# Packing the routing tasks of the last halves in a planned attention and expert kernel, and norming the last half's rows two tiles at a time

## The chip, the cores and the metric

The kernel runs on one core of a Trainium2 chip. The metric is the device time of one execution in microseconds. All engines of the core run their own instruction queues and meet by semaphores: TensorE (PE), VectorE (DVE), ScalarE (ACT), GpSimd (POOL) and SyncE (SP), which only issues transfers.

## The reference

Four sequences of 1,024 rows of 256 numbers (4,096 tokens) go through cross attention with a context, then through a mixture of experts. Cut to what matters:

```python
x = x + xattn(ctx, layernorm(x), mask, ...)     # q from x; keys and values from the context (77) and from x (1024)
h = layernorm(x)                                # "hn": the rows that are routed
scores = sigmoid(h @ gate_w.T)                  # 64 experts in 8 groups of 8
sfc = scores + gate_bias
# the 4 best groups by the sum of their two best, then the 8 best experts in them
topk_w = 2.5 * scores[topk] / (scores[topk].sum() + 1e-20)
pos = running count of an expert's tokens, in token order      # valid while pos < 256
buf[e, pos] = h[token]
y = (silu(buf @ w_gate) * (buf @ w_up)) @ w_down
out = x + sum over the valid choices of y[e, pos] * topk_w
```

Everything is in float32. An expert takes its first 256 tokens only, so the count runs through the halves in order.

## The kernel before

A sequence b has two halves x of 512 query rows, so there are eight halves, named (b, x); the last is (3,1). A half has two pairs pr of heads, and (b, x, pr) is a block. A block has 9 steps, one for each tile of 128 keys: `scores` (four matrix passes on TensorE, then `exp` on ScalarE into `probs`) and `values` (four passes into `ps_o`). Behind a block ScalarE copies the sums and the denominators out (`o_copy`, lines 1364 and 1365) and VectorE divides (`scale`, lines 1490 and 1491, in two pieces of 256 columns). A block needs the row maxima of its scores first: `max` (TensorE line 1097, VectorE line 1474) and `max_ctx`, then `neg` on VectorE, then `qb`, a transposition on TensorE (line 1124) that ScalarE copies to `qbT` (line 1334). Only then do its `scores` start.

When both blocks of a half are divided, the half is routed. Its tasks, in the order in which `route_tasks` gives them, with q one of its 4 tiles of 128 rows:

- `proj` for each tile (TensorE line 1167; VectorE lines 1496 to 1500: add to `xres`, mean and variance), then `store` (SyncE line 883: the rows go to the output)
- `hn_scale` in four pieces (VectorE: 1 / sqrt by a shift and three Newton steps, in `rsqrt`, for all four tiles at once) and `hn` for each tile (ScalarE line 1375: the normed rows into `rows`)
- `hn_turn` (TensorE line 1174, ScalarE line 1381) and `logits` (TensorE line 1180, ScalarE line 1387) for each tile
- the choice, 14 tasks on VectorE from `gates` (line 1515) to `scale_weights` (line 1598). `chosen` marks the experts, `count` adds up, `pos` (TensorE lines 1191 and 1193) gives the place of each token in its expert, `slots` and `slot_ids` make the addresses, and the last two make the weights
- 32 scatters on GpSimd (`scat`, line 956), 8 for each tile: an indirect transfer of 128 rows to `slot_rows` in memory. The first scatter of a tile waits for its choice and its normed rows.

Seven halves make one choice for their four tiles together. The last half makes four choices, one for each tile, so that its scatters can start with the first tile.

Behind the last half comes the expert stage. SyncE waits for all 256 scatters and loads the rows expert by expert (line 901); TensorE turns them and multiplies; GpSimd adds the results to the output with indirect transfers (line 1023), which wait for one another by `added0` and `added1`. The experts' weights come in three early groups: 16 behind block (2,1,1), 6 behind block (3,0,1), and 17 (line 898) behind the last block. The 17 are issued by SyncE behind the `store` of the last half, since they follow `plan.order["sp"]` in its queue.

The order of the work is made by `Plan` when the kernel is built. It puts each task in a slot (one `scores` or `values` task is a slot), beside a load in microseconds that it adds up for each engine. `route` places the routing tasks: for the halves up to (2,0) as a chain, by their costs; for (2,1) and (3,0) simply two tasks to a slot. Half (3,1) stands behind all slots. The list of all tasks gives the priorities. Then `schedule` gives each engine its own order: it takes, among the tasks whose needs (in `needs`, with assumed times) are met within 0.3 us of the soonest, the one that stands first in the list. The engines work through these orders strictly. TensorE's tasks other than `scores` and `values` share three banks of `ps_u` in turn.

## Time and profile before

| what | us |
|---|---|
| median of 3 runs | 1167.11 (1161.54 to 1170.71) |
| the profiled execution | 1164.94 |
| its span | 1163.0 |
| busy in it: PE, DVE, POOL, ACT | 945.4, 616.8, 587.2, 461.3 |
| 256 scatters (line 956), busy | 251.7, 983 ns each |
| 128 result transfers (line 1023), busy | 198.3, 1550 ns each |

The span is the time between the first and the last instruction that the profiler saw; the execution takes 1.9 us more. A row of the timeline has the start in us, the busy time in us, the engine, the line, the operation, what is written and what is read with shapes, and a count if it holds several like instructions. In brackets stand the idle time of the engine ahead of it and what ended it. "issue" means that the profile shows nothing that the engine waited for. PE is the matrix pass, PEld the load of its weights.

### The profile page before, as it was taken

The page shows a single profiled execution, that of the slowest core. Times are in us where ns is not written, and L with a number is a line of the kernel's source. Part 1 is how long each engine was busy: PE and PEld are TensorE (multiplying, and loading weights), DVE is VectorE, ACT ScalarE, POOL GpSimd, SP SyncE. Part 2 cuts the span into 40 slices and gives each one's busy share as a digit, 9 for nine tenths or more (in the row PEclk, how much of TensorE's full clock was granted, in tenths as well). Part 3 has the DMA queues.
Part 4 walks back from the last instruction along what each step waited for, and adds up shares of the span by engine and source line. Part 5 has one row for each costly group of instructions (what it writes and reads, how often), then busy time and mean ns, then how long its engine had stood idle before and what let it go on. Part 6 is the DMA issues. An engine that isn't in the chain of part 4 may idle for free.

```text
span 1163.0 us, 12926 instructions
## 1 busy us (share of the span) xinstructions
PE 945.4 (81%) x3736; PEld 598.3 (51%) x3736; DVE 616.8 (53%) x1898; ACT 461.3 (40%) x930; POOL 587.2 (50%) x530
## 2 busy tenths in 40 slices
PE   3779999999999999999999999961079977878700
PEld 1445565645655554555555545531068866666500
DVE  4473536896568776467857666647124323332300
ACT  3633665733856444566453432530023322222100
POOL 3620042307616625722853737276736667777782
PEclk9878999999999998999999998985579988998955
DMA  8519301113202323300124403015069987877668
GB/s 304 213 41 386 138 1 39 37 44 144 70 1 78 124 68 100 108 1 7 68 73 165 165 19 116 20 48 222 8 193 295 258 185 135 145 140 136 82 68 153
DMA packets 79285, 133.66 MB, mean 115 GB/s; under 512 B 13419, under 2 KB 48027, under 8 KB 79217
## 3 DMA queue, kind: packets, MB, share of 16 engines
q1 hardware_dynamic: 47345, 91.04, 23.9%
q0 software_dynamic: 31872, 41.80, 18.4%
q8 instruction: 31, 0.51, 0.2%
q14 instruction: 37, 0.30, 0.1%
HBM read 60.76 MB, written 93.00 MB: 132 GB/s over the span
## 4 chain that ended last, share of the span: by engine, by line
PE 57%; POOL 11%; issue 10%; DMA 9%; DVE 7%; ACT 4%; POOLq 0%; DVEq 0%; ACTq 0%; SPq 0%
PE ps_o L1158 22%; PE ps_u L1074 7%; PE ps_s L1142 6%; PE ps_s L1144 5%; DMA out_rows<-again,row_ids 5%; PE ps_u L1097 4%; POOL out_rows L1023 4%; POOL odd_sum L1023 3%; DMA odd_sum<-again,row_ids 3%; POOL slot_rows L956 3%; PE ps_u L1167 2%; PE ps_u L1085 2%; PE ps_u L1113 2%; PE ps_u L1124 1%; ACT den L1365 1%
## 5 line engine op out<-in xcount | busy, mean ns | idle before, releaser
L956 POOL DMA_INDIRECT slot_rows<-rows,slot_idx x256 | 251.7, 983 | 212.2 <-issue 182.7
L1474 DVE TENSOR_REDUCE mp<-ps_u 128x1 f32<-128x512 f32 x256 | 164.7, 686 | 107.4 <-PE ps_u L1097 105.7
L1348 ACT ACTIVATE probs<-ps_s 128x512 f32<-128x512 f32 x256 | 139.5, 596 | 160.0 <-PE ps_s L1144 158.5
L1158 PE MATMUL ps_o<-probs,V 128*128 128x512 f32 (+1 forms) x288 | 141.1, 614 | 2.9 <-ACT den L1365 2.9
L1158 PE MATMUL ps_o<-probs,pool 128*128 128x512 f32 (+1 forms) x288 | 140.5, 611 | 3.2 <-ACT den L1365 3.2
L971 POOL TENSOR_TENSOR pool<-pool,rs_y 128x1024 f32<-128x1024 f32 (+1 forms) x20 | 32.9, 1647 | 198.9 <-DVEq L1469 198.7
L1219 PE MATMUL ps_u<-again 128*128 128x256 f32 x512 | 130.1, 400 | 0.0
L1617 DVE TENSOR_SCALAR again<-ps_o,again 128x256 f32<-128x256 f32 x128 | 56.1, 480 | 138.8 <-DMA out_rows<-again,row_ids 79.1
L1023 POOL DMA_INDIRECT out_rows<-again,row_ids x64 | 99.2, 1550 | 53.4 <-DVE row_ids L1618 20.8
L1023 POOL DMA_INDIRECT odd_sum<-again,row_ids x64 | 99.1, 1549 | 37.0 <-issue 17.7
L1144 PE MATMUL ps_s<-qbT,Kb 65*128 65x512 f32 (+1 forms) x288 | 117.2, 407 | 0.0
L1219 PEld LDWEIGHTS ps_u<-again 128*128 128x128 f32 x512 | 99.4, 205 | 12.7 <-issue 0.3
L1074 PE MATMUL ps_u<-wqkv_s,lnT 128*128 128x512 f32 (+1 forms) x256 | 99.9, 521 | 3.0 <-ACT lnT L1271 1.9
L1394 ACT ACTIVATE again<-ps_s 128x512 f32<-128x512 f32 x64 | 38.2, 597 | 161.4 <-PE ps_s L1203 161.4
L1228 PE MATMUL ps_o<-again 128*128 128x256 f32 x256 | 71.3, 403 | 36.5 <-DVE again L1608 36.4
L1158 PEld LDWEIGHTS ps_o<-probs,V 128*128 128x128 f32 (+1 forms) x288 | 52.5, 193 | 48.0 <-issue 29.4
L1142 PE MATMUL ps_s<-Q,K 128*128 128x512 f32 x144 | 73.0, 507 | 4.3 <-ACT qbT L1334 4.3
L1158 PEld LDWEIGHTS ps_o<-probs,pool 128*128 128x128 f32 (+1 forms) x288 | 52.1, 193 | 46.8 <-issue 32.2
L1228 PEld LDWEIGHTS ps_o<-again 128*128 128x128 f32 x256 | 47.5, 194 | 52.6 <-DVE again L1608 47.0
L1203 PE MATMUL ps_s<-ident,again 128*128 128x128 f32 x256 | 41.9, 291 | 36.1 <-DMA again<-slot_rows 36.1
L1074 PEld LDWEIGHTS ps_u<-wqkv_s,lnT 128*128 128x128 f32 x256 | 49.2, 201 | 36.8 <-issue 27.1
L1490 DVE RECIPROCAL den<-den 128x256 f32<-128x256 f32 x32 | 55.9, 1747 | 17.5 <-ACT den L1365 17.1
(181 smaller groups left out, 1443.7 us busy)
## 6 DMA issues: line engine op xcount, KB each, us to landing
again<-in_wexp SPq DMA_DIRECT2D x64, 384.0 KB, 6.5
slot_rows<-rows SPq DMA_DIRECT2D x2, 10272.0 KB, 33.1
again<-slot_rows SPq DMA_DIRECT2D x64, 321.0 KB, 4.2
Kb<-K SPq DMA_DIRECT2D x16, 275.5 KB, 3.9
odd_sum<-rows SPq DMA_DIRECT2D x1, 4352.0 KB, 22.4
pool<-in_x SPq DMA_DIRECT2D x4, 1024.0 KB, 5.6
xres<-in_x SPq DMA_DIRECT2D x8, 512.0 KB, 3.8
out_rows<-xres SPq DMA_DIRECT2D x8, 512.0 KB, 3.0
```

The lines of the kernel that those rows point to most:

```text
L956: pool.indirect_dma_start(out=slot_rows, out_offset=bass.IndirectOffsetOnAxis(ap=slot_idx[x][:, q, k:k + 1], axis=0), in_=rows[x][:, q, :] ...
L1023: pool.indirect_dma_start(out=(out, odd_sum)[e % 2], out_offset=bass.IndirectOffsetOnAxis(ap=row_ids[:, e % RING, t:t + 1], axis=0), in_=y ...
L1074: i = pe.matmul(dst, lnT[0:w, at % 2, c, 0:rj], rhs, start=(c == 0), stop=(c == 1))
L1142: pe.matmul(dst, K[b % 2][:, h, kt * P:kt * P + rk], queries(b, x)[0][:, h, :], start=True, stop=False)
L1144: pe.matmul(dst, Kb[:, h, kt * P:kt * P + rk], qbT[block_no[(b, x, pr)] % 2][:, hh, :], start=False, stop=True).then_inc(s["scores_full"], 1)
L1158: i = pe.matmul(ps_o[:, hh, :], V[b % 2][0:rk, pr, kt, DH * hh:DH * hh + P], probs[0:rk, n % NPR, hh, :], start=(kt == 0), stop=(kt == NKT ...
L1219: i = pe.matmul(ps_g[:, e % 2, which, :], w_at[e % W_BUFS][:, o:o + I], xT[e % 2][:, k, :], start=(k == 0), stop=(k == 1))
L1228: i = pe.matmul(ps_y[:, e % 2, t, :], hid[e % 2][:, t * P:(t + 1) * P], w_at[e % W_BUFS][:, 4 * I:4 * I + D], start=True, stop=True)
L1348: act.activation(probs[:, n % NPR, hh, :], ps_s[:, u % NSC, :], ACT.Exp).then_inc(s["probs_made"], 1)
L1474: v.tensor_reduce(mp[:, i, tile, half:half + 1], bank((*t, i))[:, :], AX.X, ALU.max).then_inc(s["emptied_vec"], 1)
L1490: link(v.reciprocal(den[:, mine], den[:, mine]))
L1617: v.tensor_scalar(y_out[r][:, t, :], ps_y[:, e % 2, t, :], xr[r][:, t, D + 1 + e:D + 2 + e], None, ALU.mult)
```

## The change

It has four parts.

1. `route` puts four tasks of halves (2,1) and (3,0) to a slot instead of two.
2. The tasks of a half's rows are in a function of their own, `row_tasks`, for tiles q0 to q1, and `hn_scale` works on these tiles only. `NORMED` says that half (3,1) does it in two parts: tiles 0 and 1, then tiles 2 and 3.
3. The last half's list reads: first piece of the last block's `scale`, the rows of tiles 0 and 1, second piece of `scale`, the choice of tile 0 with its scatters, the rows of tiles 2 and 3, `store`, and the choices of tiles 1, 2 and 3 with theirs. Before it was: both pieces, the rows of all four tiles, the four choices.
4. In all other halves `store` stands behind `hn` in the list, not ahead of `hn_scale`.

The rest adapts `needs` and the waits: ScalarE waits for `hn_scaled` at the first tile of a part, and for `sel_made` by a part's number. `CHOSEN` is empty, so halves other than the last keep one choice.

```diff
+NORMED = {(B - 1, 1): ((0, 2), (2, 4))}
+CHOSEN = {}
...
-        for q in range(2):
-            self.add("scale", *order[-1], q)
...
-        for t in self.route_tasks(B - 1, 1, parts=[(q, q + 1) for q in range(QT)]):
+
+        rows_made = [self.row_tasks(B - 1, 1, *tiles) for tiles in NORMED[(B - 1, 1)]]
+        chosen = [[(kind, B - 1, 1, q, q + 1) for kind in CHOICE] + [("scat", B - 1, 1, q, k) for k in range(TOPK)]
+                  for q in range(QT)]
+        for t in ([("scale", *order[-1], 0)] + rows_made[0] + [("scale", *order[-1], 1)] + chosen[0] + rows_made[1]
+                  + [("store", B - 1, 1)] + chosen[1] + chosen[2] + chosen[3]):
             self.add(*t)
...
-                self.slots.setdefault(first + n // 2, []).append(t)
-            first += len(tasks) // 2
+                self.slots.setdefault(first + n // 4, []).append(t)
+            first += len(tasks) // 4
...
+    def row_tasks(self, b, x, q0, q1):
+
+        out = [("proj", b, x, t) for t in range(q0, q1)]
+        out += [("hn_scale", b, x, n, q0, q1) for n in range(4)]
+        out += [("hn", b, x, t) for t in range(q0, q1)]
+        for t in range(q0, q1):
             out.append(("hn_turn", b, x, t))
-            if t:
+            if t > q0:
                 out.append(("logits", b, x, t - 1))
...
+        return out + [("logits", b, x, q1 - 1)]
+
+    def route_tasks(self, b, x):
+        out = [t for tiles in NORMED.get((b, x), ((0, QT),)) for t in self.row_tasks(b, x, *tiles)]
+        last = out.index(("hn", b, x, QT - 1))
+        out[last + 1:last + 1] = [("store", b, x), ("residual", b, 1) if x == 0 else ("residual", b + 1, 0)]
+        for part in CHOSEN.get((b, x), ((0, QT),)):
             out += [(kind, b, x, *part) for kind in CHOICE]
         return out
...
-                    b, x, piece = t[1:]
+                    b, x, piece, q0, q1 = t[1:]
+                    mine = slice(q0, q1)
                     if piece == 0:
-                        if 2 * b + x:
+                        if 2 * b + x and q0 == 0:
                             v.wait_ge(s["hn_made"], QT * (2 * b + x))
-                        link(v.tensor_scalar(c_v[:], mvC[:, :, 1], LN_EPS, None, ALU.add))
-                    rsqrt(v, link, c_v[:], c_i[:], c_y[:], c_t[:], (piece,))
+                        link(v.tensor_scalar(c_v[:, mine], mvC[:, mine, 1], LN_EPS, None, ALU.add))
+                    rsqrt(v, link, c_v[:, mine], c_i[:, mine], c_y[:, mine], c_t[:, mine], (piece,))
```

What the plan makes of it is seen best in three places. Line numbers of the new kernel are higher, by 11 to 15.

ScalarE at the start of block (3,0,0), before: the copy of block (2,1,1) (`oT`, `den`) stands ahead of `qbT` of block (3,0,0).

```order
L1351 ACTIVATE probs<-ps_s,mask_bias 77x512 x2
L1364 ACTIVATE oT<-ps_o 64x512
L1365 ACTIVATE den<-ps_o 64x512
L1364 ACTIVATE oT<-ps_o 64x512
L1365 ACTIVATE den<-ps_o 64x512
L1334 ACTIVATE qbT<-ps_u 65x512 x2
L1348 ACTIVATE probs<-ps_s 128x512 x16
```

And in the changed kernel:

```order
L1363 ACTIVATE probs<-ps_s,mask_bias 77x512 x2
L1346 ACTIVATE qbT<-ps_u 65x512 x2
L1376 ACTIVATE oT<-ps_o 64x512
L1377 ACTIVATE den<-ps_o 64x512
L1376 ACTIVATE oT<-ps_o 64x512
L1377 ACTIVATE den<-ps_o 64x512
L1360 ACTIVATE probs<-ps_s 128x512 x12
```

`qbT` has moved ahead of the copy. On TensorE `qb` has moved ahead of the last `values` of block (2,1,1) in the same way. The same swap is at the start of block (2,0,0), and not at (3,1,0), where one pair of maxima has moved ahead of the last `values`.

VectorE in the middle of the choice of half (3,0), before: `selb` is written by `chosen`, `carry` by `count`, `wsel<-ps_u` is the first instruction that reads the positions, and `den` and `oT` are `scale` of block (3,1,0).

```order
L1556 MATCH_REPLACE rep<-v,sfc 128x64 x4
L1559 TENSOR_TENSOR selb<-rep,sfc 128x256
L1490 RECIPROCAL den<-den 128x256
L1491 TENSOR_TENSOR oT<-oT,den 128x256
L1562 TENSOR_TENSOR carry<-carry,selb 128x64 x4
L1490 RECIPROCAL den<-den 128x256
L1491 TENSOR_TENSOR oT<-oT,den 128x256
L1570 TENSOR_TENSOR wsel<-ps_u,slot_base 128x256
L1571 SCALAR_TENSOR_TENSOR rep<-ps_u,selb 128x256
```

And in the changed kernel:

```order
L1571 MATCH_REPLACE rep<-v,sfc 128x64 x4
L1574 TENSOR_TENSOR selb<-rep,sfc 128x256
L1577 TENSOR_TENSOR carry<-carry,selb 128x64 x4
L1585 TENSOR_TENSOR wsel<-ps_u,slot_base 128x256
L1586 SCALAR_TENSOR_TENSOR rep<-ps_u,selb 128x256
L1592 COPY carry<-carry 128x64
```

Both pieces of `scale` stand behind `scale_weights` now. On TensorE, all logits of the half stand ahead of `qb` of block (3,1,1) and of the `values` of step 6 of block (3,1,0); before, the last of them stood behind the `values` of step 7. Its `pos` stands ahead of the first `values` of block (3,1,1) instead of the fourth.

VectorE in the last half, before: `xres` is written by `proj`, with `bnC` and `mvC` behind it, and `c_v`, `c_i`, `c_y`, `c_t` and `c_nb` are `hn_scale`. These rows are the fourth `proj`, and what follows.

```order
L1496 TENSOR_TENSOR xres<-xres,ps_u 128x256
L1499 BN_STATS bnC<-xres 128x6
L1500 BN_AGGR mvC<-bnC 128x2
L1506 TENSOR_SCALAR c_v<-mvC 128x4
L580 TENSOR_SCALAR c_i<-c_v 128x4
L581 TENSOR_SCALAR c_y<-c_i 128x4
```

In the changed kernel, from the end of the first two tiles' `hn_scale` to the first choice (`sc` is `gates`):

```order
L1524 SCALAR_TENSOR_TENSOR c_nb<-mvC,c_y 128x2
L1510 TENSOR_TENSOR xres<-xres,ps_u 128x256
L1513 BN_STATS bnC<-xres 128x6
L1514 BN_AGGR mvC<-bnC 128x2
L1510 TENSOR_TENSOR xres<-xres,ps_u 128x256
L1513 BN_STATS bnC<-xres 128x6
L1514 BN_AGGR mvC<-bnC 128x2
L1521 TENSOR_SCALAR c_v<-mvC 128x2
L591 TENSOR_SCALAR c_i<-c_v 128x2
L592 TENSOR_SCALAR c_y<-c_i 128x2
L1530 TENSOR_SCALAR sc<-th 128x64
```

The third and fourth `proj` stand behind `hn_scale` of the first two tiles. The second piece of `hn_scale` of tiles 2 and 3 stands between `count` and `pos` of the first choice, and the last two pieces stand behind that choice. In this part of the program the orders of GpSimd and SyncE are the same in both kernels.

## Rows read from the trace of the kernel before

**Rows 1.** The page, its first line.

```profile
span 1163.0 us, 12926 instructions
```

**Rows 2.** The timeline of GpSimd and of SyncE's queue, from the scatters of (3,0) on.

```profile
758.54 0.99 POOL L956 DMA_INDIRECT slot_rows<-rows,slot_idx  x1 [18.46 <-issue]
...
799.33 0.98 POOL L956 DMA_INDIRECT slot_rows<-rows,slot_idx  x1 [5.02 <-issue]
...
842.08 0.98 POOL L956 DMA_INDIRECT slot_rows<-rows,slot_idx  x1 [1.96 <-issue]
...
845.93 0.98 POOL L956 DMA_INDIRECT slot_rows<-rows,slot_idx  x1 [0.30 <-issue]
848.09 3.90 SPq L901 DMA_DIRECT2D again<-slot_rows  x8
```

**Rows 3.** The timeline of GpSimd in the scatters of half (2,1).

```profile
727.79 0.98 POOL L956 DMA_INDIRECT slot_rows<-rows,slot_idx  x1 [3.16 <-issue]
```

**Rows 4.** DMA queues in 780 to 786, 786 to 794, and the loads' queue in 799.3 to 803.

```profile
q0 software_dynamic: 90, 0.13, 9.7%
...
q0 software_dynamic: 308, 0.04, 3.4%
...
q1 hardware_dynamic: 281, 0.74, 52.2%
```

**Rows 5.** The timeline of VectorE and TensorE, choice of half (3,0).

```profile
740.73 0.29 DVE L1515 TENSOR_SCALAR sc<-th 128x256 f32<-128x256 f32 x1 [8.11 <-ACT th L1387]
...
747.92 1.75 DVE L1490 RECIPROCAL den<-den 128x256 f32<-128x256 f32 x1
...
748.38 1.88 PE L1158 MATMUL ps_o<-probs,V 128*128 128x512 f32 x4
...
751.04 1.88 PE L1158 MATMUL ps_o<-probs,V 128*128 128x512 f32 x4
...
753.19 0.42 DVE L1570 TENSOR_TENSOR wsel<-ps_u,slot_base 128x256 f32<-128x256 f32 x1 [0.16 <-PE ps_u L1193]
```

**Rows 6.** The timeline of the last half: VectorE, and the weight loads.

```profile
770.71 1.75 DVE L1490 RECIPROCAL den<-den 128x256 f32<-128x256 f32 x1 [13.00 <-ACT den L1365]
...
778.05 0.42 DVE L1496 TENSOR_TENSOR xres<-xres,ps_u 128x256 f32<-128x256 f32 x1
...
780.06 10.30 SPq L898 DMA_DIRECT2D again<-in_wexp  x17
...
780.31 0.17 DVE L1506 TENSOR_SCALAR c_v<-mvC 128x4 f32<-128x4 f32 x1
...
782.71 0.16 DVE L1509 SCALAR_TENSOR_TENSOR c_nb<-mvC,c_y 128x4 f32<-128x4 f32 x1
...
786.77 0.20 DVE L1515 TENSOR_SCALAR sc<-th 128x64 f32<-128x64 f32 x1 [3.90 <-ACT th L1387]
...
794.30 0.15 DVE L1598 COPY rows<-token_id 128x1 f32<-128x1 f32 x1
```

**Rows 7.** The timeline at the starts of blocks (2,0,0), (3,0,0) and (3,1,0).

```profile
445.32 0.50 PE L1142 MATMUL ps_s<-Q,K 128*128 128x512 f32 x1 [2.50 <-ACT qbT L1334]
...
624.26 1.04 PE L1124 MATMUL ps_u<-ident,QL 128*65 128x128 f32 x8
...
624.46 0.59 ACT L1364 ACTIVATE oT<-ps_o 64x512 f32<-64x512 f32 x1 [3.36 <-PE ps_o L1158]
...
626.89 1.07 ACT L1334 ACTIVATE qbT<-ps_u 65x512 fp32r<-65x512 f32 x2
...
628.02 0.50 PE L1142 MATMUL ps_s<-Q,K 128*128 128x512 f32 x1 [1.81 <-ACT qbT L1334]
...
696.15 2.48 DVE L1474 TENSOR_REDUCE mp<-ps_u 128x1 f32<-128x512 f32 x4 [1.06 <-PE ps_u L1097]
```

**Rows 8.** Windows: length, busy PE, PEld, DVE, ACT, POOL, PEclk, DMA share, GB/s.

```profile
446.00:453.00 7.00, 7.00 (x14) 3.50 (x13) 3.85 (x5) 2.88 (x5) 5.44 (x6) 0.51 0.37 131
...
698.00:709.00 11.00, 10.17 (x28) 6.82 (x27) 6.75 (x11) 3.70 (x7) 8.56 (x9) 0.53 0.61 213
```

More of the change, by code:

```diff
@@ L154, in __init__ @@
                     self.add(*t)
-        for t in self.route_tasks(B - 1, 1, parts=[(q, q + 1) for q in range(QT)]):
+        rows_made = [self.row_tasks(B - 1, 1, *tiles) for tiles in NORMED[(B - 1, 1)]]
[3 more added lines that the diff above has]
+                  + [("store", B - 1, 1)] + chosen[1] + chosen[2] + chosen[3]):
             self.add(*t)
-            if t[0] == "scale_weights":
-                for k in range(TOPK):
-                    self.add("scat", B - 1, 1, t[3], k)
         self.schedule()
@@ L270, in add, with normed_with @@
         self.tasks.append((kind, *args))
-    def route_tasks(self, b, x, parts=((0, QT),)):
-        out = [("proj", b, x, t) for t in range(QT)]
-        out += [("store", b, x)] + [("hn_scale", b, x, n) for n in range(4)]
-        out += [("hn", b, x, t) for t in range(QT)]
-        if (b, x) != (B - 1, 1):
-            out.append(("residual", b, 1) if x == 0 else ("residual", b + 1, 0))
-        for t in range(QT):
+    def row_tasks(self, b, x, q0, q1):
[3 more added lines that the diff above has]
+        for t in range(q0, q1):
             out.append(("hn_turn", b, x, t))
-            if t:
+            if t > q0:
                 out.append(("logits", b, x, t - 1))
-        out.append(("logits", b, x, QT - 1))
-        for part in parts:
+        return out + [("logits", b, x, q1 - 1)]
[4 more added lines that the diff above has]
+        for part in CHOSEN.get((b, x), ((0, QT),)):
             out += [(kind, b, x, *part) for kind in CHOICE]
         return out
+    def normed_with(self, b, x, q):
+        return next(k for k in NORMED.get((b, x), ((0, QT),)) if k[0] <= q < k[1])
     def needs(self, t):
@@ L395, in needs @@
             yield "dve", 1.15, [(*t, "pe"), ("residual", b, x, "pool")] + (
-                [("hn_scale", c, y, 3, "dve")] if b + x else [])
+                [("hn_scale", c, y, 3, *self.normed_with(c, y, QT - 1), "dve")] if b + x else [])
         elif kind == "store":
@@ L399, in needs @@
         elif kind == "hn_scale":
-            b, x, piece = t[1:]
+            b, x, piece, q0, q1 = t[1:]
             c, y = (b, 0) if x else (b - 1, 1)
-            yield "dve", 0.65, [("proj", b, x, q, "dve") for q in range(QT)] + (
-                [("hn_scale", b, x, piece - 1, "dve")] if piece else
+            yield "dve", 0.65, [("proj", b, x, q, "dve") for q in range(q0, q1)] + (
+                [("hn_scale", b, x, piece - 1, q0, q1, "dve")] if piece else
                 [("hn", c, y, q, "act") for q in range(QT)] if b + x else [])
@@ L406, in needs @@
             b, x, q = t[1:]
-            yield "act", 0.42, [("hn_scale", b, x, 3, "dve")] + (
+            yield "act", 0.42, [("hn_scale", b, x, 3, *self.normed_with(b, x, q), "dve")] + (
                 [("scat", b - 1, x, QT - 1, TOPK - 1, "pool", 3.5)] if b else [])
@@ L425, in needs @@
             elif n == 0 and b + x:
-                done.append((CHOICE[-1], c, y, 0, QT, "dve"))
+                done.append((CHOICE[-1], c, y, *self.part_of[(c, y, QT - 1)], "dve"))
             if kind == "pos":
@@ L749, in program @@
     pos_units = [u for u in units if u[0] == "pos"]
+    scaled_no = {(t[4], *t[1:3]): n for n, t in enumerate(t for t in plan.tasks if t[0] == "hn_scale" and t[3] == 3)}
     part_no = {(*u[1:3], q): n for n, u in enumerate(pos_units) for q in range(u[3], u[4])}
```

11 lines of the change are left out of this document (6 added, 5 removed).

## The prediction

> **What bounds the kernel now.** I read the page first, then the timeline of GpSimd around the end of attention, then the instructions that feed it, and last the stretches in which TensorE waits or runs slowly. The span is 1163.0 us [rows 1]. It has two stages. In attention (up to the last `values` task) TensorE is busy nearly all the time. In the expert stage TensorE starts only when every routed row stands in `slot_rows`: SyncE issues the first load of rows at 848.09, directly behind the last scatter of GpSimd, which starts at 845.93 and takes 0.98 [rows 2]. From there to the end are 314.9 us that the change does not touch. So the question is when the last scatter ends.
>
> GpSimd issues the scatters of half (3,0) and then those of (3,1), 64 in all, from 758.54 on. They stand 1.285 us apart. The run has two gaps that are larger: 5.02 us before 799.33 and 1.96 us before 842.08 [rows 2]. The first comes behind the 28th scatter of (3,0), the second 32 scatters later. The same gap stands behind 28 scatters of half (2,1), with 3.16 us [rows 3]. I read it as a ring of 32 scatters: at its end GpSimd waits until the scatters under way have landed. Quiet, that costs about 2 us; in the 5.02 us case the 17 weight loads issued from 780.06 were running. In their first 6 us the scatters' queue moved 90 packets, 15 per us; in the next 8 us it moved 308, 38 per us [rows 4], which is what scatters 1.285 us apart ask for (49 each). So loads starve the scatters at first, and the backlog is gone only slowly. GpSimd, from 758.54 on, is thus the path, and what starts it is the choice of half (3,0).
>
> **The choice of (3,0): 8.7 us earlier.** Before, `gates`, the first step of the choice, waits 8.11 us for the last logits and starts at 740.73 [rows 5]. In the new order `qb`, two `values` tasks and one `scores` task that stood ahead of these logits stand behind them. A `scores` with its `values` takes 2.66 us (748.38 to 751.04 [rows 5]), a second `values` 1.9 and `qb` 1.04 [rows 7]: 5.6 us together. The normed rows must be ready in time for that. `hn_scale` now runs in one piece, with fewer maxima between its steps, which brings them about as much forward. I take 5.2 us, since TensorE may then wait a little for the first of them. Next: before, two `scale` tasks (one reciprocal 1.75 us and one product each, from 747.92) stood inside the choice; it reads the positions at 753.19 [rows 5], and 5.35 us later GpSimd starts. Now the choice runs as one piece and the scales stand behind it; nobody waits for them until the copy of the last block, 20 us later. From 747.92 to the positions it was 5.3 us; the two reciprocals (3.5 us) and about 0.4 of the products go from it, 3.9 us, and the count and the positions' matmul remain. TensorE reaches that matmul only behind the first `scores` tasks of the next block, which gives 0.4 us back. So 5.2 + 3.9 - 0.4 = 8.7: GpSimd starts at 749.8.
>
> **The gap at the ring's end: 0.5 us given back.** 28 scatters at 1.285 bring the gap to 785.8 instead of 794.3. Where are the weights then? They are issued behind the store of the last half, which waits for the fourth `proj`. That `proj` now stands behind the first two tiles' `hn_scale`, which takes from 780.31 to 782.87 [rows 6], 2.6 us, so the loads start at 782.7. The gap would fall 3 us into them, into the worst part. The backlog is then 3 us of (38 - 15), some 70 packets, and the scatter just issued, 49: 45 of them leave in the slow 3 us that remain, the rest at 38 per us in 1.9 us, and landing takes 0.4: a gap of 5.3 us. GpSimd goes on at 791.1 instead of 799.33, 8.2 us earlier. Bounds: with a gap of 2 us, as the quiet one, it goes on at 787.8 (11.5 earlier); if it waits until all 17 loads are in (about 21 us from their start), at 804, 4.7 later than before. I stay near the 5.02 us row, the one taken under the same loads.
>
> The 36 scatters that remain take 47.6 us from 799.33 on, with one quiet gap [rows 2]; the gap's place behind the loads is kept, so they cost the same. They need the first choice of (3,1) when four of them are done, at 796.2. Before, it is ready at 794.45 [rows 6]. Now two `proj` rounds (778.05 to 780.31, 2.26 us [rows 6]) leave its path, and one `hn_scale` piece of 0.6 us enters between count and positions, where VectorE waits for the matmul anyway. That makes 792.3: no wait. The later choices cost 7.6 us each (786.77 to 794.45 [rows 6]) and the next one 1.4 us more, against 10.3 us for eight scatters: covered. Without the split the choice would stand at 794.5, still ahead of 796.2, so by itself the split buys nothing with my gap, and 1.6 us with a quiet one. Its 13 more small VectorE instructions lie beside GpSimd and cost nothing; what it does cost is that the loads start 2.6 us later, which is in the gap above.
>
> A page bears on this and speaks against it. The Trainium skill, "SBUF — State Buffer", section "SBUF: two separate sides", says that GpSimd cannot write descriptors while VectorE holds the port pair that they share, so that choices beside scatters would stretch them. The trace does not agree: the scatters stand 1.285 us apart with VectorE idle (758.54 to 770.71) and with its choices running (799.33 on) [rows 2, 6]. By that rule the sum would be smaller by an amount that no row gives; I use the row.
>
> **Attention: 6.5 us earlier.** The end of attention moves all of the above. The `values` and `scores` tasks are the same in number, so only waits of TensorE can go. There are three places, each at the start of a block. At 624.46 ScalarE copies the finished block out, and only then, at 626.89, the `qb` result; TensorE stands 1.81 us and starts at 628.02 [rows 7]. In the new order `qb` is ahead of the last `values` on TensorE and ahead of the copy on ScalarE. Then `scores` follow the last `values` without a wait and the next `values` wait only for the copy: 2.3 us less. The same swap stands at block (2,0,0), where TensorE stands 2.50 us [rows 7]: again 2.4. At (3,1,0) four reductions (2.48 us from 696.15 [rows 7]) are between the last `values` and `qb`; one pair of them (1.3 us) has moved ahead: 1.3. The denser rows (three `proj` in a row, four logits in a row) can make TensorE wait for banks: minus 1. Sum 5.0, bounds 0 and 6.
>
> At two of the three places the clock fell just after the wait: 0.51 in 446 to 453 and 0.53 in 698 to 709, the lower level of 1.2 GHz [rows 8]; at 628, after 1.81 us, it did not. Half clock over 7 and 10 us of dense work costs 3.4 and 5. With shorter waits one of these may go; another may come where order is new. I add 1.5 us, with bounds of -4 and +8. The Trainium skill ("TensorE: Matmul & The Clock Gate", "What's actually happening") says the same from the other side: idleness throttles the clock and activity releases it. By that rule, taken strictly, both dips go, which is the upper bound; the row at 628 shows that a wait alone does not settle it.
>
> **Sum.** 8.2 (GpSimd against the end of attention) + 5.0 + 1.5 = 14.7 us. 1163.0 - 14.7 = 1148.3 of span; the execution took 1164.94, 1.9 above its span, so 1150.2. From the median of the three runs, 1167.11, it is 1152.4. I forecast 1151.
>
> **Rivals.**
> 1. *The gap swallows the loads.* GpSimd cannot go on before the weights are in. For it: in the first 6 us the scatters' queue got two fifths of its rate. Against: before, it went on at 799.33 while 281 load packets were still to come [rows 4]. Price: -4.7 instead of +8.2; the total gain is 1.8 and the time 1164. Chance 0.12.
> 2. *Attention does not gain.* The waits move elsewhere, since VectorE is nearly full around the packed rows, and a dip stays at each place. 1163.0 - 8.2 + 1.9, or 1159 from the median: about 1158. Chance 0.18.
> 3. *Both gains in full.* Quiet gap and both dips gone: 11.5 + 6 + 8 = 25: 1141. Chance 0.13.
> 4. *The swap turns against the kernel.* `qb` now stands ahead of the last `values` in TensorE's order. If the maxima end late, because a choice holds VectorE (it holds it 7.2 us up to `chosen`, 740.73 to 747.92 [rows 5]), TensorE stands with that `values`, the copy and the next block behind it. From a delay of some 4 us at each of the two swaps it eats the gain; with 6 us each and two further dips (3.4 and 5) it is 20 us lost against 8.2 won: 1178. For it: VectorE has to be through with the maxima one `values` earlier than before. Against: the positions of the choice (0.9 us), which stood ahead of the last maximum, stand behind it now. Chance 0.07.
> My forecast has 0.50.
>
> Range: 1140 holds rival 3, 1161 holds rival 2; rivals 1 and 4 are left out. About 1% (11.7 us) is what a measurement here can tell from no change, so faster means below 1155.4. That takes the forecast, rival 3 and a little of rival 2: 0.68; the same holds the rest of 2, rival 1 and the upper edge of the forecast: 0.25; slower is rival 4: 0.07.
>
> **What would show it.** Take the first `scale` of the last block as the mark, 770.71 before [rows 6]. Right: it starts 5 to 8 us earlier; GpSimd's first scatter of (3,0) lies 20.9 us ahead of it instead of 12.2; the gap behind the 28th is 4 to 6 us and ends 20.4 us behind the mark instead of 28.6; no wait of TensorE above 1 us at blocks (2,0,0) and (3,0,0); the expert stage still lasts 315 us. Wrong: the gap lasts until the loads end; scatters of (3,1) wait for a choice; or TensorE waits on `neg` ahead of a last `values`.

## The result, and the profile after

| | before | changed |
|---|---|---|
| median, both on one chip | 1164.29 (12 runs, 1158.56 to 1170.71 and one of 1864.83) | 1153.24 (12 runs, 1148.72 to 1160.55) |
| ratio, 95% interval | | 0.9907 [0.9878, 0.9937] |
| the profiled execution | 1164.94 | 1154.19 |
| its span | 1163.0 | 1152.2 |

The changed kernel is 0.9% faster, 11 us. The forecast was 1151 in a range of 1140 to 1161.

The same view as in [rows 2], GpSimd and SyncE's queue, of the changed kernel:

```profile
747.63 0.99 POOL L968 DMA_INDIRECT slot_rows<-rows,slot_idx  x1 [15.89 <-issue]
...
790.07 0.99 POOL L968 DMA_INDIRECT slot_rows<-rows,slot_idx  x1 [6.77 <-issue]
...
832.88 0.98 POOL L968 DMA_INDIRECT slot_rows<-rows,slot_idx  x1 [1.96 <-issue]
780.19 9.64 SPq L910 DMA_DIRECT2D again<-in_wexp  x17
838.89 12.33 SPq L913 DMA_DIRECT2D again<-slot_rows  x9
```

The first scatter of (3,0) starts 10.9 us earlier than before, the rows are loaded 9.2 us earlier. Between the two stands the gap behind the 28th scatter, now 6.77 us instead of 5.02. From the load to the end are 313.3 us (314.9 before).

VectorE, answering to [rows 5, 6]:

```profile
742.28 0.42 DVE L1585 TENSOR_TENSOR wsel<-ps_u,slot_base 128x256 f32<-128x256 f32 x1 [1.06 <-PE ps_u L1205]
746.63 0.17 DVE L1613 COPY rows<-token_id 128x4 f32<-128x4 f32 x1
746.70 1.75 DVE L1504 RECIPROCAL den<-den 128x256 f32<-128x256 f32 x1
768.34 1.75 DVE L1504 RECIPROCAL den<-den 128x256 f32<-128x256 f32 x1 [17.31 <-ACT den L1377]
778.10 0.16 DVE L1524 SCALAR_TENSOR_TENSOR c_nb<-mvC,c_y 128x2 f32<-128x2 f32 x1
788.71 0.15 DVE L1613 COPY rows<-token_id 128x1 f32<-128x1 f32 x1
```

The choice of (3,0) ends at 746.80 (746.63 and 0.17), then come the two `scale` tasks that stood inside it before. The mark, the first `scale` of the last block, is at 768.34: only 2.4 us earlier than before. The first choice of the last half is ready at 788.86.

The runs are best compared stage by stage. In this table "opening" is the start of the first `values` task; attention goes from there to the mark; the next three columns tell of the last half, in us behind the mark (negative: ahead of it); the last stage goes from the first load of rows to the end of the span. Every entry is a difference of two starts in the timeline of one profiled execution. The lower rows belong to the experiments.

| kernel | opening | attention | first scatter of (3,0) | gap: length, end | rows loaded | last stage | span |
|---|---|---|---|---|---|---|---|
| before | 96.11 | 674.60 | -12.2 | 5.02, 28.6 | 77.4 | 314.9 | 1163.0 |
| changed | 96.45 | 671.89 | -20.7 | 6.77, 21.7 | 70.6 | 313.3 | 1152.2 |
| e5: without the split | 93.99 | 672.22 | -20.7 | 5.08, 20.0 | 68.8 | 314.1 | 1149.1 |
| e6: `store` alone | 94.40 | 673.70 | -13.9 | 5.16, 27.1 | 75.8 | 317.4 | 1161.3 |
| e7: loads held back | 93.66 | 672.16 | -20.7 | 1.91, 16.9 | 65.7 | 312.5 | 1144.0 |
| e11: and `store` old in b = 0 | 96.52 | 668.38 | -20.7 | 1.91, 16.9 | 65.7 | 311.7 | 1142.3 |
| e12: e7 without the split | 94.34 | 672.14 | -20.7 | 1.90, 16.9 | 68.2 | 317.4 | 1152.1 |

Two things are seen at once. Where the code is the same the columns in the middle repeat to 0.1 us, attention to 0.3. The opening (93.7 to 96.5) and the last stage (311.7 to 317.4) spread by 3 and 6 us though their code is the same in all of them. So the 1.6 us that the changed kernel's last stage is shorter are not put down to the change, and experiments are read from the middle columns; the totals carry this spread on top.

TensorE's waits in 300 to 770, before and changed ("engine, what it writes, line, waited for: us in total, times, longest"):

```profile
PE ps_s L1142 <- ACT qbT L1334: 5.0, 3, 2.5
PE ps_o L1158 <- ACT den L1365: 5.0, 6, 1.6
PE ps_u L1097 <- DVE mp L1474: 2.0, 3, 1.3
```

```profile
PE ps_u L1097 <- DVE mp L1488: 4.4, 3, 2.4
PE ps_o L1170 <- ACT den L1377: 2.1, 3, 1.3
PE ps_u L1109 <- DVE mp L1488: 1.8, 2, 1.3
PE ps_u L1186 <- ACT th L1401: 1.5, 2, 0.7
PE ps_s L1154 <- ACT probs L1360: 1.2, 2, 0.9
PE ps_u L1109 <- ACT hnT L1394: 1.1, 1, 1.1
PE ps_s L1154 <- ACT qbT L1346: 0.7, 1, 0.7
```

(L1097 in the changed kernel is the transposition that stood on L1085, L1109 the `max` of L1097.) The waits on `qbT` and `den` fell from 10.0 to 2.8 us, as meant. All others, 3.3 us before (two groups not shown have 1.3), came to 11.0 (three not shown have 1.0): what the swaps took away has come back as waits on the maxima and on the routing's own chain. In all, TensorE's waits in this window are 13.3 us before and 13.8 changed, so it is not by shorter waits that attention became 2.7 us shorter. The windows from the first `values` to the mark, before and then changed (columns as in [rows 8]), tell where it comes from:

```profile
96.11:770.71 674.60, 654.03 (x2453) 370.13 (x2451) 441.77 (x1268) 350.08 (x703) 292.29 (x296) 0.98 0.24 80
```

```profile
96.45:768.34 671.89, 650.56 (x2453) 368.67 (x2451) 448.08 (x1268) 350.04 (x703) 298.55 (x303) 0.98 0.24 81
```

The same number of passes keeps TensorE busy for 3.5 us less: less of the dense work falls into stretches at the lower clock.

### The profile page after: what moved, and what is told of

The parts are those of the page before. It is cut to its first block, busy times and chain, and to the rows that moved or that the text cites. A ratio compares the mean times of both kernels' runs of the same rounds, so it can differ in the third digit from the quotient of the medians.

```text
span 1152.2 us, 12929 instructions
## 1 busy us (share of the span) xinstructions
PE 938.2 (81%) x3736; PEld 592.8 (51%) x3736; DVE 624.7 (54%) x1911; ACT 461.7 (40%) x930; POOL 587.0 (51%) x530
## 4 chain that ended last, share of the span: by engine, by line
PE 56%; DMA 11%; POOL 10%; issue 10%; DVE 8%; ACT 4%; POOLq 0%; DVEq 0%; ACTq 0%; SPq 0%
PE ps_o L1170 21%; DMA out_rows<-again,row_ids 7%; PE ps_u L1086 7%; PE ps_s L1154 6%; PE ps_s L1156 5%; PE ps_u L1109 4%; POOL out_rows L1035 4%; POOL odd_sum L1035 3%; PE ps_u L1179 2%; PE ps_u L1097 2%; DMA odd_sum<-again,row_ids 2%; PE ps_u L1125 2%; POOL slot_rows L968 2%; PE ps_u L1136 1%; PE ps_u L1192 1%
## 5 line engine op out<-in xcount | busy, mean ns | idle before, releaser
L1231 PE MATMUL ps_u<-again 128*128 128x256 f32 x512 | 126.7, 392 | 0.0
L1231 PEld LDWEIGHTS ps_u<-again 128*128 128x128 f32 x512 | 96.9, 200 | 11.8 <-issue 0.3
L1086 PEld LDWEIGHTS ps_u<-wqkv_s,lnT 128*128 128x128 f32 x256 | 49.6, 202 | 36.5 <-issue 27.1
```

Source lines behind the costliest of these rows:

```text
L1086: i = pe.matmul(dst, lnT[0:w, at % 2, c, 0:rj], rhs, start=(c == 0), stop=(c == 1))
L1231: i = pe.matmul(ps_g[:, e % 2, which, :], w_at[e % W_BUFS][:, o:o + I], xT[e % 2][:, k, :], start=(k == 0), stop=(k == 1))
```

## Experiments

The chips were of two kinds. In the result above and on the chips of e5 to e7, e11 and e12 the kernel before takes 1160 to 1164 us; on three other chips (e1 to e4; e8 and e9; e10) it takes 1293 to 1303, with the same code and inputs. The second kind is told of in the last section; its times are given, but no theory is settled by them.

**e1 to e4: the parts one by one.** All four on a chip of the second kind. The edits: e1 is the kernel before with

```diff
-                self.slots.setdefault(first + n // 2, []).append(t)
-            first += len(tasks) // 2
+                self.slots.setdefault(first + n // 4, []).append(t)
+            first += len(tasks) // 4
```

e2 is the kernel before with the line of part 4 alone:

```diff
-        out += [("store", b, x)] + [("hn_scale", b, x, n) for n in range(4)]
-        out += [("hn", b, x, t) for t in range(QT)]
+        last = (b, x) == (B - 1, 1)
+        out += [("store", b, x)] * last + [("hn_scale", b, x, n) for n in range(4)]
+        out += [("hn", b, x, t) for t in range(QT)] + [("store", b, x)] * (not last)
```

e3 has both of these edits and no split; e4 is the changed kernel with `n // 2` and the old place of `store`, so the split alone.

> The kernel before with part 1 alone: halves (2,1) and (3,0) get four routing tasks to a slot; `store` stays ahead of `hn_scale`, and the last half's rows stay in one part. In this order TensorE has the four `proj` of (3,0) ahead of `qb` of block (3,1,0), and no swap of `qb` at blocks (2,0,0) and (3,0,0).
> Theory A (each part works by itself, packing frees the choice): the first scatter of (3,0) is about 20 us ahead of the first `scale` of the last block instead of 12.2, the gap behind the 28th falls about 3 us ahead of or at the start of the weight loads' worst part, attention ends within 1 us of before: 7 to 8 us faster than before, ratio 0.993 to 0.994.
> Rival B (packing needs the other place of `store`): TensorE stands several us at the start of block (3,1,0), because `proj` ahead of `qb` waits for what is not there yet; attention ends 3 to 8 us later and eats the gain: ratio 0.998 to 1.002.

> The kernel before with part 4 alone: `store` stands behind `hn` in all halves but the last. This gives the swap of `qb` with the last `values` at blocks (2,0,0) and (3,0,0), and with it all changes of order up to half (2,0).
> Theory A (the swaps buy attention time; the forecast's terms 2.3 and 2.4 us and the clock): the last block's first `scale` starts 4 to 6 us earlier than before and the whole is as much faster: ratio 0.995 to 0.997.
> Rival C (the waits only move, as the changed kernel's trace suggests, where attention got 2.4 us shorter, and that behind block (3,0,0)): attention ends within 1.5 us of before, ratio 0.998 to 1.001, with new waits of TensorE on VectorE's maxima in blocks (1,0,1) and (2,0,1).

> The changed kernel without the split: parts 1 and 4 as in the changed kernel, the last half's rows normed in one part as before (parts 2 and 3 undone).
> Theory A (the split buys nothing with a gap this long; it only delays the weight loads): the same as the changed kernel within 1 us; the loads start about 2.6 us earlier, ahead of or with the gap, which is then 5 to 6 us and ends at the same place within 1 us; ratio to before 0.990 to 0.992.
> Rival D (the split is what carries the last half): the scatters of (3,1) wait 2 to 4 us for their first choice; ratio to before 0.993 to 0.995.

> The kernel before with the split alone (parts 2 and 3): two tasks to a slot and the old place of `store` in the other halves. The orders up to the end of attention are those of before.
> Theory A: nothing gained, since the first choice of (3,1) was ready ahead of need before; the weight loads start 2 us later than before and the gap behind the 28th scatter falls otherwise into them by that much; within 1 us of before, ratio 0.999 to 1.001.
> Rival D (the earlier choice is used): 2 to 3 us faster, ratio 0.997 to 0.998.

| | median | ratio to before (1293.61 there) |
|---|---|---|
| e1 packing | 1300.59 | 1.0041 [1.0005, 1.0078] |
| e2 `store` | 1294.15 | 1.0013 [0.9982, 1.0044] |
| e3 both | 1294.79 | 1.0009 [0.9978, 1.0040] |
| e4 split | 1290.25 | 0.9987 [0.9948, 1.0026] |

None of the expected ratios was made for a kernel that takes 1293 us. Only e1 has an interval that does not hold 1, and by very little, on the slower side. Its trace has the place that rival B names: from the last `values` of block (3,0,1) to the first of (3,1,0) go 45.4 us against 19.6 to 30.6 in e2, e3 and e4, and 10.6 us of that are idle time of TensorE ahead of `proj`, which in e1 stands ahead of `qb`; the other three have none there. On such a chip that is a hint and not a price. Packing alone was not tried on the first kind of chip, and neither was the split alone. e3 and e2 were run again (e5, e6).

**e5: the changed kernel without the split.** The edit of e3. Before took 1162.87 on this chip, which e6 and e7 share.

> The same kernel as in e3 (the changed one with the last half's rows normed in one part), again, because in the first job every kernel, the one before too, took about 1293 us, with all engines idle for 5 to 13 us at a time while scatters ran.
> On a chip where the kernel before takes about 1165 us: theory A (the split buys nothing at the length of the gap; it delays the weight loads): the loads start 2 to 3 us earlier than in the changed kernel, the gap ends within 1 us of where it did there (21.7 us behind the first `scale` of the last block), total within 1 us of 1153, ratio 0.989 to 0.992. Rival D (the split carries the last half): the scatters of (3,1) wait 1 to 3 us for their first choice, ratio 0.992 to 0.994.
> Where the kernel before takes 1293 us again: nothing to be read from the ratio.

1150.42 us, ratio 0.9888 [0.9858, 0.9918]. No scatter of (3,1) waited for its choice, so rival D falls. The weight loads start at 9.25 us behind the mark instead of 11.85, just the 2.6 us of the forecast. But the gap does not end at the same place: it begins 5.7 us into the loads, not 3.1, and is 5.08 us, not 6.77, so the rows are loaded 1.7 us earlier than with the split. At this length of the gap the split costs 1.7 us; theory A had it at zero. This is read from the middle columns of one execution of each kernel: the ratios of the two kernels (0.9888 and 0.9907) cannot be told apart.

**e6: `store` alone.** The edit of e2.

> The same kernel as in e2 (the one before with the new place of `store` alone), again for the same reason.
> On a chip where the kernel before takes about 1165 us: theory A (the swaps of `qb` buy attention time, terms 2.3 and 2.4 us and the clock): the last block's first `scale` starts 4 to 6 us earlier than 770.7, ratio 0.995 to 0.997. Rival C (the waits only move): it starts within 1.5 us of 770.7, ratio 0.998 to 1.001, with waits of TensorE on the maxima in blocks (1,0,1) and (2,0,1) as in the changed kernel's trace.

1161.02 us, ratio 0.9980 [0.9957, 1.0004]. From the first `values` to the mark are 673.70 us against 674.60: 0.9 us gained, not 4 to 6. Its waits of TensorE in 300 to 770:

```profile
PE ps_u L1086 <- DVE mp L1475: 4.4, 3, 2.4
PE ps_o L1159 <- ACT den L1366: 2.3, 3, 1.6
PE ps_u L1098 <- DVE mp L1475: 2.0, 3, 1.3
```

They are those of the changed kernel: rival C, the waits moved. Against before the start of `values` is -0.1 us in block (1,0,0), +3.3 from step 1 of block (1,0,1) to block (1,1,0), -1.4 from step 1 of (2,0,0) on, +1 to +7.5 in (2,0,1), where the order of the tasks differs most, -0.5 at step 0 of (3,0,0) and -2.4 at step 1 of (3,1,0) (each counted from the first `values`). Up to block (3,0,0) the changed kernel follows the same line to within 0.3 us (0.6 at one step). So all that attention gains and loses up to there comes from the place of `store`, none from the packing. In the last block e6 loses 1.7 us again, behind a wait of 1.57 us on `den` at 741.36 with 3.4 us at the lower clock after it, and the changed kernel does not. e5, which has no split, does not either (672.22 us), so that much, 1.8 us of the 2.7, is the packing's.

e6 also tells the parts of the earlier choice apart. With `store` alone the first scatter of (3,0) is 13.9 us ahead of the mark, before 12.2, with the packing too (e5) 20.7. So the place of `store` brings 1.7 of the 8.5 us and the packing the other 6.8: in e6 both `scale` tasks still stand inside the choice.

**e7: the weight loads held back.** The changed kernel with one line more, ahead of the loop of the 17 loads:

```diff
             wait_block(sp, (B - 1, 1, PR - 1))
+            sp.wait_ge(s["scattered0"], B * HALF_SCATTERS)
```

> The changed kernel, with the last 17 weight loads held back until all scatters of (3,0) have landed, so that the gap behind the 28th scatter falls into quiet queues.
> Theory A (the gap is the wait at the ring's end, 2 us quiet, and what lies above it is the loads' doing): the gap is 2.0 us instead of 6.8, GpSimd goes on 4.8 us earlier, the first choice of (3,1), ready 20.5 us behind the mark, is then about 0 to 1 us late or just in time; the first load of rows is 4 to 4.8 us earlier; but the loads of the first experts' weights may now be late in the expert stage. If they are not, ratio 0.986 to 0.988 to before.
> Rival E (the gap has another cause, for example the half's end or its choice): it stays near 6 us wherever the loads are; ratio 0.990 to 0.992.

1147.26 us, ratio 0.9868 [0.9839, 0.9897].

```profile
782.68 0.98 POOL L969 DMA_INDIRECT slot_rows<-rows,slot_idx  x1 [1.91 <-issue]
...
825.51 0.98 POOL L969 DMA_INDIRECT slot_rows<-rows,slot_idx  x1 [1.96 <-issue]
788.65 8.94 SPq L911 DMA_DIRECT2D again<-in_wexp  x17
831.53 12.85 SPq L914 DMA_DIRECT2D again<-slot_rows  x9
```

With nothing beside it the gap is 1.91 us and ends 16.9 us behind the mark; the rows are loaded 4.8 us earlier (65.7 against 70.6), as theory A has it to 0.1 us. The last stage (312.5 us) does not show that it misses the weights, whose loads now start 11.0 us later against the mark. Rival E falls. What made the gap long was the loads: nothing else was changed. The scatters' queue shows what GpSimd waits for. In the changed kernel 1344 of its packets start from the first scatter of (3,0) to the end of the gap, 48 for each of the 28 scatters issued, so not one is outstanding when GpSimd goes on; in e7 it is the same number.

**e8, e10 and e11: `store` back at its old place in the first sequence.** The kernel of e7 with

```diff
-        out[last + 1:last + 1] = [("store", b, x), ("residual", b, 1) if x == 0 else ("residual", b + 1, 0)]
+        out[last + 1:last + 1] = [("store", b, x)] * (b > 0) + [("residual", b, 1) if x == 0 else ("residual", b + 1, 0)]
+        if b == 0:
+            out.insert(QT, ("store", b, x))
```

> The kernel of e7 (the changed one with the weight loads held back) with `store` at its old place in halves (0,0) and (0,1), at the new one in all others. This gives TensorE the old order in blocks (0,1,0) to (1,0,1) and keeps both swaps of `qb`, at (2,0,0) and (3,0,0).
> Theory A (the new place of `store` costs in the first halves what it wins at the swaps: every trace with part 4 is 3.4 us behind the kernel before from block (1,0,1) on, with a wait of TensorE on the maxima of 2.4 us and a stretch at the lower clock behind it): the 3.4 us at (1,0,1) go, and the whole is 3 to 4 us faster than e7: 1143 to 1144.5, ratio 0.983 to 0.985.
> Rival F (the waits and the lower clock turn up at the next tight place instead; attention has no slack to give): within 1 us of e7, ratio 0.986 to 0.988.

Twice it came to a chip of the second kind: 1285.25 us, ratio 0.9926 [0.9884, 0.9967], and 1296.88 us, 0.9956 [0.9919, 0.9993]. The third time it met one of the first:

> The same kernel as in e8 and e10 once more (weight loads held back, `store` at its old place in halves (0,0) and (0,1)), since both were taken where the kernel before takes about 1300 us and only the sign could be read.
> On a chip where the kernel before takes about 1165 us: theory A: the `values` tasks from block (1,0,1) to (1,1,0) are where the kernel before has them, 3.4 us earlier than in the changed kernel, and the whole is 1143 to 1144.5, ratio 0.983 to 0.985. Rival F: within 1 us of e7, ratio 0.986 to 0.988, the waits and the lower clock at another place.
> Where it takes about 1300 us: ratio below 1 again, and no more to be read.

1145.26 us against 1159.78 for before on that chip: ratio 0.9877 [0.9853, 0.9902], not the 0.983 to 0.985 of theory A. The trace tells why. Block (1,0,1) in the changed kernel, TensorE's waits and the `values` of step 0; then the same in e11:

```profile
314.73 0.50 PE L1109 MATMUL ps_u<-K,Q1b 64*128 64x512 f32 x2 [1.11 <-ACT hnT L1394]
...
316.97 1.11 PE L1097 MATMUL ps_u<-ident,st 128*128 128x128 f32 x4 [1.15 <-DVE mp L1488]
...
318.62 2.78 PE L1170 MATMUL ps_o<-probs,V 128*128 128x512 f32 x4
```

```profile
314.95 0.66 PE L1100 MATMUL ps_u<-ident,st 128*128 128x128 f32 x4 [0.18 <-DVE mp L1491]
...
316.05 1.94 PE L1173 MATMUL ps_o<-probs,V 128*128 128x512 f32 x4
```

The first wait is gone, 0.18 us is left of the second, and the lower clock behind them is gone too. The windows, changed kernel and then e11 (columns as in [rows 8]):

```profile
316.90:320.30 3.40, 3.33 (x10) 2.44 (x11) 3.37 (x5) 2.19 (x5) 2.48 (x2) 0.50 0.00 0
```

```profile
316.90:320.30 3.40, 3.40 (x18) 2.12 (x17) 3.33 (x5) 2.92 (x8) 0.00 (x0) 1.00 0.00 0
```

Up to block (1,1,0) the `values` of e11 start where those of the kernel before do, within 0.1 us; at step 1 of (2,0,0) they are 5.0 us ahead, and attention is 6.2 us shorter than before and 3.8 shorter than in e7. That is theory A's mechanism and its size. But its opening took 96.5 us, e7's 93.7, so of the 4.6 us that the execution is shorter from the first `values` on, the span shows 1.7, the medians 2.0, and the ratios of e7 and e11 cannot be told apart. Rival F falls by the trace; by the times alone it could not.

**e9: a larger scratch memory for GpSimd's descriptors.** The changed kernel with `dynamic_dma_scratch_size=4608` in place of 4096.

> The changed kernel with the scratch memory for GpSimd's descriptors set to 4608 bytes for each partition instead of 4096, nothing else.
> Theory A (a ring that 4096 bytes make 32 scatters long, at whose end GpSimd waits for the scatters under way): the gaps now stand 36 scatters apart instead of 32. In the last 64 scatters one falls ahead of the 21st of (3,0), before the weight loads, one ahead of the 25th of (3,1), behind them; both are 2 us. The 6.8 us go: the whole is 4 to 5 us faster than the changed kernel, 1147 to 1149.5, ratio 0.986 to 0.988.
> Rival E (the gap belongs to the half, its choice or the loads, not to a ring): it stays behind the 28th scatter of (3,0) with 5 to 7 us; ratio 0.989 to 0.992.

On the second kind of chip: 1286.35 us, ratio 0.9965 [0.9937, 0.9992]. The places of the gaps can be read there too. Apart from the starts of halves, the changed kernel's gaps of over 1.9 us stand before scatters 29, 61, 93 and so on to 253; with 4608 they stand before 32, 64, 96 and so on to 256. The distance is 32 in both, and only the start moved, by three. So theory A's distance of 36 did not come, and rival E's fixed place behind the 28th did not either. But every half has 32 scatters, so "every 32 scatters" and "once in each half, behind the 28th, or the 31st with the larger memory" are the same thing here, and no run tells them apart. For the second reading: 31 to 28 is 1.11 and 4608 to 4096 is 1.125, as if a store of that size were filled anew in each half. Something does grow with the memory: among the 128 result transfers, 1.55 us each, slightly longer ones (1.56 and 1.57) recur every 15 with 4096 and every 17 with 4608. What sets the place of the gap stays open, and the time that theory A gave was not tested on a chip of the first kind.

**e12: does the split pay where the gap is quiet?** e7 with the edit of e3.

> The kernel of e7 (weight loads held back, gap of 1.9 us that ends 16.9 us behind the first `scale` of the last block) without the split: the last half's rows are normed in one part, all else as there.
> On a chip where the kernel before takes about 1160 us: theory A (the split pays only where the gap is quiet, as the prediction's 1.6 us): the first choice of (3,1) is ready 23.7 us behind the mark, its first scatter is wanted at 22.0, so GpSimd waits some 1.8 us for it and the rows are loaded 1.7 us later than in e7 (67.4 us behind the mark instead of 65.7): ratio 0.988 to 0.989 against 0.987 there.
> Rival G (the split costs or gains somewhere else, in the loads or the later choices): 65.7 or less, or above 69.
> Where the kernel before takes about 1300 us: only the places of the gaps can be read.

1151.20 us against 1163.53: ratio 0.9890 [0.9863, 0.9916].

```profile
783.35 0.98 POOL L958 DMA_INDIRECT slot_rows<-rows,slot_idx  x1 [1.90 <-issue]
...
787.20 0.98 POOL L958 DMA_INDIRECT slot_rows<-rows,slot_idx  x1 [0.30 <-issue]
791.02 0.98 POOL L958 DMA_INDIRECT slot_rows<-rows,slot_idx  x1 [2.84 <-issue]
```

The first scatter of (3,1) now waits: 2.84 us of idle time where e7 has 0.30. The rows are loaded 68.2 us behind the mark, 2.5 later than in e7, somewhat more than the 1.7 expected, because from the end of the choice (790.19) to the scatter go another 0.8 us. Rival G's bounds (65.7 or less, or above 69) did not come. So the split is worth 2.5 us in e7 and costs 1.7 in the changed kernel, both read from when the rows are loaded; the span of e12 has on top a last stage of 317.4 us.

## Why the forecast was right, step by step

**Bound and last stage.** Right: every us that the last scatter came earlier came out at the end; the last stage stayed, within its own spread.

**The choice of (3,0), 8.7 us.** Right: first scatter 20.7 us ahead of the mark, forecast 20.9. `gates` starts at 733.17, which is 35.2 us ahead of the mark instead of 30.0: the 5.2 us of the forecast. From there to the positions go 9.1 us instead of 12.5, 3.4 against the forecast's 3.5: no `scale` stands between, and the positions waited 1.06 us for TensorE (0.16 before), the price put at 0.4. By e6 and e5 most of it, 6.8 us, comes with the packing.

```profile
733.17 0.29 DVE L1530 TENSOR_SCALAR sc<-th 128x256 f32<-128x256 f32 x1 [0.26 <-ACT th L1401]
```

**The gap, 0.5 us given back.** Right in kind, 1.5 us too small: 6.77 instead of 5.3, ended 21.7 behind the mark instead of 20.4. The 8.2 us became 6.9. The packets of the scatters' queue in the changed kernel, in 783.30 to 786.19 (up to 6 us from the loads' start) and in 786.19 to 788.65, tell which terms:

```profile
q0 software_dynamic: 62, 0.02, 2.6%
...
q0 software_dynamic: 82, 0.00, 2.1%
```

From 788.65 to the end of the gap at 790.07 the queue moves nothing. So 144 packets were outstanding and not 119; 62 of them left in the slow stretch and not 45; the other 82 took 2.4 us and not 1.9, at the rate that the forecast had (79 of them in 2 us). And from the last packet to the scatter go 1.5 us, where the forecast put 0.4 for landing: that term is the one that failed, with 1.1 of the 1.5 us. It is no matter of the loads: in the quiet gap of e7 it is 1.1 us too. The runs give the gap by how far it begins into the loads:

| begins after the loads' start by | length |
|---|---|
| 3.1 us (changed) | 6.77 |
| 5.7 (e5) | 5.08 |
| 12.1 (e6) | 5.16 |
| 14.3 (before) | 5.02 |
| no loads yet (e7) | 1.91 |

Two traces of the second kind of chip fit in: 5.37 us at 5.2 (e4) and 4.98 at 6.0 (e2). The 6.77 at 3.1 stands in one trace only.

Its bounds, 2 us and the end of the loads, held: e7 is the lower one, and rival 1 did not come true, since GpSimd went on 9.9 us behind the loads' start, when SyncE had only just issued the last of them (9.64 us).

**The split.** "By itself the split buys nothing with my gap, and 1.6 us with a quiet one": e5 and e12 say -1.7 and +2.5. Right in sign for the quiet gap; with the long one the delay of the loads, counted in the forecast, was not set against it in this sentence.

**VectorE's port.** The rule of the Trainium skill ("SBUF — State Buffer", "SBUF: two separate sides"), that GpSimd cannot write descriptors while VectorE holds the port pair that they share, is once more not seen: in e7 the scatters from 782.68 on stand 1.28 us apart with the first choice of (3,1) on VectorE beside them, up to 786.37. Whether any of the choice's instructions holds that pair no row tells.

```profile
783.97 0.98 POOL L969 DMA_INDIRECT slot_rows<-rows,slot_idx  x1 [0.30 <-issue]
785.25 0.98 POOL L969 DMA_INDIRECT slot_rows<-rows,slot_idx  x1 [0.30 <-issue]
786.53 0.98 POOL L969 DMA_INDIRECT slot_rows<-rows,slot_idx  x1 [0.30 <-issue]
```

**Attention, 6.5 us.** This is the step that failed: 2.7 us (671.89 against 674.60). Of its two terms the waits, 5.0 us, gave nothing in sum (13.3 us before, 13.8 after), and the clock, 1.5 us, gave more than it was put at: TensorE was busy 3.5 us less. Yet the three places did what was forecast. The start of block (3,0,0), changed kernel:

```profile
624.50 1.07 ACT L1346 ACTIVATE qbT<-ps_u 65x512 fp32r<-65x512 f32 x2 [1.70 <-PE ps_u L1136]
...
626.59 0.59 ACT L1376 ACTIVATE oT<-ps_o 64x512 f32<-64x512 f32 x1 [1.02 <-PE ps_o L1170]
...
629.67 0.50 PE L1154 MATMUL ps_s<-Q,K 128*128 128x512 f32 x1 [0.30 <-ACT probs L1360]
```

The wait of 1.81 us is 0.30. At (2,0,0) 4.9 us were won between block (1,1,0) and step 1 of (2,0,0), 2.4 for the wait and the rest for the dip of [rows 8] that did not come back: its longest wait there is 0.92 us and the granted clock stays at its upper level of 2.4 GHz. At (3,1,0) the wait is 0.68 and the dip is 7 us long, not 10.

```profile
442.00:453.00 11.00, 10.08 (x38) 5.38 (x36) 9.66 (x24) 7.31 (x15) 4.15 (x5) 1.00 0.35 97
501.20:504.60 3.40, 3.40 (x11) 2.15 (x9) 3.37 (x4) 1.32 (x4) 2.09 (x2) 0.50 0.00 0
699.00:706.00 7.00, 6.32 (x16) 4.11 (x15) 4.56 (x5) 3.57 (x6) 5.29 (x6) 0.51 0.75 262
```

What failed is the sentence "there are three places". The move of `store` also changed the order in blocks (0,1,0) to (1,0,1), where no term stood. There it costs 3.4 us (2.3 of waits and a stretch at 1.2 GHz), and between the ends of blocks (2,0,0) and (2,1,0) another 1.0, with a second new dip behind a wait of 2.35:

```profile
500.88 0.84 PE L1097 MATMUL ps_u<-ident,st 128*128 128x128 f32 x4 [2.35 <-DVE mp L1488]
```

e11 shows it: with the first sequence's order put back, attention is 6.2 us shorter than before. The term of 1.5 us for the clock had named such a dip ("another may come where order is new") at the right size, but as one in exchange for one, not with the waits ahead of it; two of 3.4 us came, against 6.8 us that went at (2,0,0) and 3.4 at (3,1,0). The Trainium skill's rule on the clock ("TensorE: Matmul & The Clock Gate", "What's actually happening") is that idleness throttles and activity releases; it agrees with these rows in that each of the new dips stands right behind idle time, and the 0.92 us at (2,0,0) has none behind it.

**Sum.** Forecast 8.2 + 5.0 + 1.5 = 14.7. Measured in the traces: 6.9 behind the mark, 2.7 in attention, -0.3 in the opening, 1.6 in the last stage, 10.8 in all. So 3.8 of attention and 1.3 of the gap are missing, and 1.3 of chance stands against them. Rival 2 (attention does not gain, 1158) was nearer for that one term than the forecast; rivals 1, 3 and 4 did not come. That the time, 1153.24, is only 2 us from the 1151 of the forecast owes something to luck: the first three runs of the kernel before, from which it was counted, had their median at 1167.11, and all twelve have it at 1164.29. By the medians the gain is 11 us, not 14.7.

## What to carry to other kernels

A change of a task's place in a list that a planner orders moves more than the places it was made for: compare the orders from the program's start, and price each stretch that differs, the ones with new waits above all. Ahead of a wait for transfers under way, keep bulk loads out of the queues: one wait that held 17 loads back by 11 us bought 4.8 us, and no cost showed beyond the spread of the last stage. Whether an earlier result is worth anything is decided by what else its consumer waits for, so the same split was worth 2.5 us beside a short gap and -1.7 beside a long one. The best kernel here, e7's with `store` at its old place in the first sequence, takes 1145 us.

## What the runs showed of the hardware that was not expected

GpSimd stops once in each run of 32 scatters, behind the 28th (behind the 31st with the larger scratch memory), until every packet of the scatters issued so far has been moved, and goes on 1.1 to 1.9 us after the last of them. Mostly that takes 1.9 to 2.7 us, up to 6.8 with loads under way; the stop of half (2,1) took 4.0 and 4.1 us in e7 and e11 without such loads, which is not explained.

On the second kind of chip every kernel takes 1285 to 1303 us. e10 and e11 are the same kernel on either kind. The opening (93.70 and 96.52 us), one scatter (0.98 us) and the last stage (311.4 and 311.7) are alike; from the first scatter to the 65th go 217.0 us instead of 184.7. In e10 VectorE goes on standing idle when the matrix pass that it needs is done, and in ten cases what ends the wait is given as "remote" (in e11 in none):

```profile
DVE mp L1491 <- remote: 73.0, 10, 13.4
```

```profile
270.46 0.49 PE L1112 MATMUL ps_u<-K,Q 64*128 64x512 f32 x1
273.15 0.69 DVE L1491 TENSOR_REDUCE mp<-ps_u 128x1 f32<-128x512 f32 x1 [6.84 <-remote]
281.61 0.69 DVE L1491 TENSOR_REDUCE mp<-ps_u 128x1 f32<-128x512 f32 x1 [5.64 <-remote]
297.81 1.41 DVE L1491 TENSOR_REDUCE mp<-ps_u 128x1 f32<-128x512 f32 x2 [13.42 <-PE ps_u L1112]
```

The first pass is done at 270.95, and VectorE takes it up at 273.15. The three waits stand in the first burst of scatters, between 256 and 298 us; the third, the longest, is put down to TensorE. What holds the engines there was not tried and stays open. The gain seems smaller on such a chip (e8 and e10: 0.4 to 0.7% where e11 has 1.2%).
